# Graph attention and a mixture of experts on one core: weighted sums in pairs, and the shared steps in a new order

## The chip, the core and the metric
The kernel runs on one core of a Trainium2 chip. The metric is the device time of one execution in microseconds, lower is better. Engines: PE (TensorE: matmuls; its weight loads are listed apart as PEld), DVE (VectorE), ACT (ScalarE), POOL (GpSimd), SP (SyncE, here only a DMA queue and its waits). All five follow programs of their own and meet at semaphores.

## What is computed
Four graphs of 256 nodes go through two layers of an 8-head graph attention, which updates `x`; then every token goes to two of 16 experts and to a shared expert. Cut to what matters:

```python
def gat_layer(x, adj, W, a_self, a_neigh, b):
    feat = jnp.einsum('nf,hfo->hno', x, W)
    e = (feat*a_self).sum(-1)[:, :, None] + (feat*a_neigh).sum(-1)[:, None, :]
    e = leaky_relu(e, 0.2) + MASK_VAL * (1.0 - adj)
    return elu(softmax(e) @ feat + b)                 # heads side by side
x = x + tanh(g_xattn) * gat_layer(gat_layer(ctx, layernorm(x), ...), ...)
flat = layernorm(x);  logits = flat @ router_w.T     # top 2 of 16, with weights
for e in range(16): out += combine[:, e] * (silu(flat@Wu[e]) * (flat@Wg[e])) @ Wd[e]
out += (silu(flat @ Su) * (flat @ Sg)) @ Sd            # the shared expert
x = x + tanh(g_ffn) * out
```

## The kernel before
**Attention.** The work is cut into eight units, (graph, layer): four graphs of layer 0, then four of layer 1. A unit has four pairs of heads. For pair `j` of unit `k`, PE's `edges(k, j)` spreads the row terms into one of two PSUM banks, DVE's `edge` turns them into masked, unnormalised weights in `prob` (two operations a head, some 0.41 us each), and PE's `weighted(k, j)` multiplies them with the features into `ps_pv`. The two heads of a pair use the two halves of the array's columns, 64 apart, side by side. `prob` has four slots for a head each, so DVE's write for pair `j` waits for the sums of pair `j - 2`; an `edges` waits for DVE to have read the pair two before it.

Between these lies the rest of the neighbouring units: `own_maxima(k+1)` (one column, after DVE's row maxima), `turn_pv(k-1)` (eight transpositions of the sums of the unit before), `features(k+1)`, `spread_t(k+1)`, `rows(k+2)` (projections) and `turn_z(k-1)` (only where the unit before is of layer 0). ACT's order in unit `k` is fixed: `evict_h1` (the turned output of two units ago, behind `turn_z`), `evict_pv(k-1, 1)` (the upper half of the sums, out of PSUM), `row_exps(k+1)` (seven small operations in a chain), ELU, three evictions, `evict_pv(k, 0)`. POOL then makes `rows_r`, for which the next unit's first `edges` waits. `turn_pv` waits for both halves of `evict_pv`:

```python
def turn_pv(k):
    for half in range(2):
        pe.wait_ge(pv_out[half], k + 1)
```
The loop runs over units 0 to 5; units 6 and 7 are written out, interleaved with normalisation and router of the first graphs.

**Router.** For each graph, `route`, DVE's top two, `ranks` (PE counts who came before) and `positions` give each token a row in a DRAM table; POOL scatters the tokens there. After graph 3 DVE makes the table of tiles (`tables`), PE turns it (`turn_table`), `whole_tables` writes it as integers, SP reads it and loads the first tiles, once the scatters have landed. `warm(n)` are `n` idle matmuls.

**Shared expert.** Eight steps `s`, two for a graph: `up(s)` on PE, `gate_tanh(s)` on ACT, `shared_step(s)` on DVE (two operations), `down(s)` on PE into `ps_acc`. Steps 0 to 3 run among the router's work, 4 to 7 behind the expert tiles. `base(g)` adds the result of graph `g` to `x_res`.

**Tiles and tail.** 24 tiles of two experts' 64 rows each; then each token's two results are read back (`y_got`), `bring(g, k)` adds them on DVE, and SP stores.

Of the kernel before, what the change touches and what calls it, by code (L numbers as in the profile page):

```python
# [13 lines left out]
P = 128  # L14
HEADS, F_OUT = 8, 32
# [21 lines left out]
def flamingo_block(nc, x, ctx_t, gates, w0, w1, a_self, a_neigh, b0, b1, router_t, router_bias,  # L37
# [13 lines left out]
    EARLY = SHARED_STEPS // 2  # L51
# [12 lines left out]
    with ExitStack() as ctx:  # L64
        def sb(name, shape, dt=F32):
            return ctx.enter_context(nc.sbuf_tensor(name, shape, dt))
# [4 lines left out]
        def sem(name):  # L71
# [66 lines left out]
        prob = sb("prob", [P, 4, C, N])  # L138
# [60 lines left out]
        y_got = [t[:].rearrange("p a c n -> p (a c n)").rearrange("p (g k f) -> p g k f", g=2, k=TOP)[:, i]  # L199
                 for t in (prob, mask_t) for i in range(2)]  # L200
# [320 lines left out]
        def _(act):  # L521
# [216 lines left out]
            gate_tanh(2)  # L738
            gate_tanh(3)
# [10 lines left out]
            for s in range(EARLY, SHARED_STEPS - 2):  # L750
                gate_tanh(s)
# [4 lines left out]
            for s in range(SHARED_STEPS - 2, SHARED_STEPS):  # L756
                gate_tanh(s)

        @block.vector
        def _(dve):  # L760
# [96 lines left out]
            def edge(k, h):  # L857
                a, i = UNITS[k]
                n = HEADS * k + h
                dve.wait_ge(edge_ready, n // 2 + 1)  # L860
                if h == 0:
                    dve.wait_ge(t_nat_ready, k + 1)
                    dve.wait_ge(mask_t_ready, a + 1)
                if n >= 4:
                    dve.wait_ge(pv_done, n // 2 - 1)
                for c in range(C):
                    last = dve.scalar_tensor_tensor(prob[:, n % 4, c, :], ps_edge[n // 2 % 2][:, h % 2, :],  # L867
                                                    t_nat[:, k % 2, c, 0, h:h + 1], mask_t[:, a, c, :],
                                                    ALU.max, ALU.mult)
                last.then_inc(p_done, 1)  # L870
# [274 lines left out]
            for j in range(W_AHEAD):  # L1145
                pick_weights(j, of_tile[j])
            base(1)
# [8 lines left out]
            for s in range(EARLY, SHARED_STEPS - 1):  # L1156
                shared_step(s)
# [3 lines left out]
            shared_step(SHARED_STEPS - 1)  # L1161
# [3 lines left out]
            base(B - 1, range(T - 1))  # L1165
# [5 lines left out]
        def _(pe):  # L1171
# [80 lines left out]
            def weighted(k, j):  # L1252
                n = PAIRS * k + j
                pe.wait_ge(p_done, 2 * (n + 1))
                if j == 0:
                    pe.wait_ge(feat_ready, k + 1)
                    if k == 0:
                        pe.wait_ge(pv_zeroed, 1)
                if j % 2 == 0 and k:
                    pe.wait_ge(pv_out[j // 2], k)  # L1260
                for c in range(C):
                    for h in range(2 * j, 2 * j + 2):
                        at = 64 * (h % 2)
                        last = pe.matmul(ps_pv[at:at + HO, j, :], feat[:, k % 2, c, h, :],  # L1264
                                         prob[:, (HEADS * k + h) % 4, c, :], start=(c == 0), stop=(c == C - 1))
                last.then_inc(pv_done, 1)
# [57 lines left out]
            def task(k, j):  # L1324

                before, after, later = k - 1, k + 1, k + 2
                if j == 0 and 0 <= before < NU:
                    turn_pv(before)
                if j == 1 and after < NU:
                    features(after)  # L1330
                    spread_t(after)
                if j == 1 and k in MASK_SLOT:
                    turn_mask(MASK_SLOT[k])
                if j == 2 and later < NU:
                    rows(later)
                if j == 3 and graph_after(before, 0) is not None:
                    turn_z(before, graph_after(before, 0))

            def up(s, ks=range(2)):
                g, e = s // SHARED, EXPERTS + s % SHARED  # L1340
                if EARLY <= s < EARLY + 2:
                    pe.wait_ge(h_done, TILES)
# [38 lines left out]
            def tile_up(j):  # L1381
                pe.wait_ge(picked, j + 1)
                pe.wait_ge(xt_out, j + 1)
                if j >= 2:
                    pe.wait_ge(h_done, j - 1)
                for c in range(C):
# [110 lines left out]
            down(2)  # L1497
            warm(8)
            turn_tile(0)
            down(3)  # L1500
            for j in range(TILES + 2):
# [8 lines left out]
                if 0 <= j - 2 < TILES:  # L1510
                    tile_down(j - 2)
            for s in range(EARLY, SHARED_STEPS):
                up(s)
                if s > EARLY:
                    down(s - 1)
            down(SHARED_STEPS - 1)
# [51 lines left out]
```

## Time and profile before
| what | value |
|---|---|
| median of 3 runs | 206.76 us (202.15 to 207.87) |
| the profiled execution | 201.63 us, of which the span of instructions is 199.5 us |
| PE | 172.8 us busy, 87% of the span |
| DVE | 153.5 us, 77% |
| ACT | 96.1 us, 48% |
| POOL | 79.8 us, 40% |
| mean granted TensorE clock | 0.978 |
| chain that ended last | PE 70%, DVE 17%, issue 5% |

The share of busy time is a mean over stages with different limits: attention (to 104 us, with the router of the first graphs inside its last units), router and shared steps (to 134 us), tiles (to 182 us) and tail. The start and the length of single operations come from the timeline; an x8 behind a row joins eight instructions of one line, and its length is that from the first one's start to the last one's end. A matmul of 32-bit floats shows as two passes, so `weighted` shows as x8, `up` as x8 and `down` as x4. The time in square brackets is how long the engine stood idle before, and what released it.

### The profile page before, as it was taken

The page shows a single profiled execution, that of the slowest core. Times are in us where ns is not written, and L with a number is a line of the kernel's source. Part 1 is how long each engine was busy: PE and PEld are TensorE (multiplying, and loading weights), DVE is VectorE, ACT ScalarE, POOL GpSimd, SP SyncE. Part 2 cuts the span into 40 slices and gives each one's busy share as a digit, 9 for nine tenths or more (in the row PEclk, how much of TensorE's full clock was granted, in tenths as well). Part 3 has the DMA queues.
Part 4 walks back from the last instruction along what each step waited for, and adds up shares of the span by engine and source line. Part 5 has one row for each costly group of instructions (what it writes and reads, how often), then busy time and mean ns, then how long its engine had stood idle before and what let it go on. Part 6 is the DMA issues. An engine that isn't in the chain of part 4 may idle for free.

```text
span 199.5 us, 4043 instructions
## 1 busy us (share of the span) xinstructions
PE 172.8 (87%) x1137; PEld 115.1 (58%) x1137; DVE 153.5 (77%) x491; ACT 96.1 (48%) x252; POOL 79.8 (40%) x116
## 2 busy tenths in 40 slices
PE   0286999999999999998997985499999999998962
PEld 0065456566767675665765774395555555545841
DVE  6986999989989899989997875728676676740494
ACT  2063647594888383866118320005566565653100
POOL 8067563512141414342275574300545455455000
PEclk9999999999999999999999999679999999999997
DMA  3799999999999940000031021223444444411684
GB/s 128 216 395 430 424 420 424 416 414 424 288 357 350 412 194 0 3 0 2 0 109 55 14 102 71 83 80 81 132 150 129 147 126 146 127 61 79 184 316 158
DMA packets 18358, 38.13 MB, mean 191 GB/s; under 512 B 2785, under 2 KB 13602, under 8 KB 16162
## 3 DMA queue, kind: packets, MB, share of 16 engines
q1 hardware_dynamic: 15488, 31.25, 43.7%
q0 software_dynamic: 1920, 5.26, 7.0%
q10 hardware_dynamic: 930, 1.38, 1.9%
q8 instruction: 9, 0.15, 0.3%
q14 instruction: 11, 0.09, 0.1%
HBM read 14.53 MB, written 23.35 MB: 190 GB/s over the span
## 4 chain that ended last, share of the span: by engine, by line
PE 70%; DVE 17%; issue 5%; ACT 3%; POOL 2%; another core or an unknown queue 1%; POOLq 0%; DVEq 0%; ACTq 0%
PE ps_pv L1264 15%; PE ps_edge L1389 12%; PE ps_edge L1248 6%; PE ps_pv L1410 5%; PE ps_nat L1378 4%; PE ps_edge L1347 4%; PE ps_feat L1228 4%; PE ps_nat L1275 4%; DVE prob L867 3%; PE ps_rows L1211 2%; PE ps_nat L1190 2%; PE ps_nat L1185 2%; PE ps_pv L1358 2%; DVE x_res L1050 2%; PE ps_nat L1237 1%
## 5 line engine op out<-in xcount | busy, mean ns | idle before, releaser
L867 DVE SCALAR_TENSOR_TENSOR prob<-ps_edge,t_nat,mask_t 128x256 f32<-128x256 f32 x128 | 54.0, 477 | 3.3 <-PE ps_edge L1248 2.3
L487 POOL DMA_INDIRECT y_tok<-pv_t,y_row x24 | 23.1, 963 | 33.8 <-DVE y_row L1018 21.5
L1264 PE MATMUL ps_pv<-prob,feat 128*33 128x256 f32 x256 | 35.2, 397 | 0.6 <-issue 0.5
L1389 PE MATMUL ps_edge<-up_w,xt 128*64 x96 | 25.9, 392 | 0.0
L1389 PE MATMUL ps_edge<-up_now,xt 128*64 128x256 f32 x96 | 25.9, 392 | 0.0
L1264 PEld LDWEIGHTS ps_pv<-prob,feat 128*33 128x33 f32 x256 | 12.5, 113 | 12.3 <-issue 4.1
L1248 PE MATMUL ps_edge<-rows_r,sel_row 128*128 128x256 f32 x64 | 16.7, 348 | 1.8 <-DVE prob L867 1.5
L416 POOL TENSOR_TENSOR rows_r<-rows_q,rows_h 128x256 fp32r<-128x256 f32 x8 | 5.9, 731 | 30.9 <-ACT rows_h L549 30.9
L479 POOL DMA_INDIRECT x_rows<-x_hat,pos x12 | 12.2, 1019 | 10.2 <-DVE pos L955 7.1
L1248 PEld LDWEIGHTS ps_edge<-rows_r,sel_row 128*128 128x128 f32 x64 | 10.3, 205 | 9.8 <-issue 5.3
L1347 PE MATMUL ps_edge<-x_t,up_w 128*128 128x256 f32 x64 | 15.5, 385 | 0.0
L1389 PEld LDWEIGHTS ps_edge<-up_w,xt 128*64 128x64 f32 x96 | 11.2, 136 | 7.4 <-issue 3.8
L1410 PE MATMUL ps_pv<-down_w,x_less 128*64 x48 | 14.4, 381 | 1.1 <-issue 0.6
L670 ACT ACTIVATE xt<-ps_nat 128x256 f32<-128x256 f32 x24 | 9.1, 379 | 12.4 <-PE ps_nat L1378 12.2
L1034 DVE SCALAR_TENSOR_TENSOR mask<-mask,ps_edge 128x128 f32<-128x128 f32 x24 | 6.9, 287 | 10.0 <-ACT mask L676 9.3
L1410 PE MATMUL ps_pv<-down_now,x_less 128*64 128x256 f32 x48 | 14.4, 381 | 0.0
L688 ACT ACTIVATE pv_t<-ps_pv,mask_t 128x256 f32<-128x256 f32 x24 | 11.4, 475 | 5.1 <-PE ps_pv L1410 3.4
L676 ACT ACTIVATE mask<-ps_edge 128x128 f32<-128x128 f32 x24 | 6.7, 278 | 14.0 <-PE ps_edge L1389 8.2
L1347 PEld LDWEIGHTS ps_edge<-x_t,up_w 128*128 128x128 f32 x64 | 11.8, 190 | 2.6 <-issue 1.2
L569 ACT ACTIVATE pv_t<-ps_pv 128x512 f32<-128x512 f32 x16 | 9.5, 597 | 6.8 <-PE ps_pv L1264 6.8
L1025 DVE COPY up_now<-up_w 128x512 f32 x24 | 10.1, 421 | 1.8 <-issue 1.8
L1358 PE MATMUL ps_pv<-down_w,a_all 128*128 128x256 f32 x32 | 9.6, 425 | 2.2 <-issue 1.3
(188 smaller groups left out, 381.6 us busy)
## 6 DMA issues: line engine op xcount, KB each, us to landing
x_rows<-x_t SPq DMA_DIRECT2D x16, 1024.0 KB, 16.4
mask_t<-x_rows SPq DMA_DIRECT2D x48, 64.5 KB
up_w<-in_wu SPq DMA_DIRECT2D x1, 2048.0 KB, 30.3
up_w<-in_wg SPq DMA_DIRECT2D x1, 2048.0 KB, 11.2
down_w<-in_wd SPq DMA_DIRECT2D x1, 2048.0 KB, 10.1
x_res<-in_x SPq DMA_DIRECT2D x3, 256.0 KB, 3.7
out<-x_res SPq DMA_DIRECT2D x3, 256.0 KB, 2.1
prob<-y_tok SPq DMA_DIRECT2D x2, 256.0 KB, 3.4
```

The costliest lines, as they stand in the source:

```text
L479: pool.indirect_dma_start(x_rows[:], bass.IndirectOffsetOnAxis(pos[:, a, k, t:t + 1], 0), rows_of[a][:, k, t, :], None).then_inc(scattered ...
L487: pool.indirect_dma_start(y_tok[:], bass.IndirectOffsetOnAxis(y_row[:, j % R_SLOTS:j % R_SLOTS + 1], 0), y_sb[:, j % Y_SLOTS, :], None).th ...
L569: act.activation(pv_t[:, 2 * half:2 * half + 2], ps_pv[:, 2 * half:2 * half + 2], ACT.Copy).then_inc(pv_out[half], 1)
L688: act.activation(y_sb[:, j % Y_SLOTS], ps_y[j % 2], ACT.Copy, scale=x_in[:, j % X_SLOTS, D + 1:D + 2]).then_inc(y_ready, 1)
L867: last = dve.scalar_tensor_tensor(prob[:, n % 4, c, :], ps_edge[n // 2 % 2][:, h % 2, :], t_nat[:, k % 2, c, 0, h:h + 1], mask_t[:, a, c, ...
L1025: mark(dve.tensor_copy(up_now[:, j % W_SLOTS].rearrange("p k f -> p (k f)"), up_w[:, bass.ds(e, 1), :, :].rearrange("p s k f -> p (s k f)")))
L1248: last = pe.matmul(ps_edge[n % 2][:, h % 2, :], sel_row[:, h, :], rows_r[:, k % 2, :], start=True, stop=True)
L1264: last = pe.matmul(ps_pv[at:at + HO, j, :], feat[:, k % 2, c, h, :], prob[:, (HEADS * k + h) % 4, c, :], start=(c == 0), stop=(c == C - 1))
L1347: last = pe.matmul(ps_edge[s % 2][:, k, :], up_w[:, e, k, c * P:(c + 1) * P], x_t[:, g, c, :], start=(c == 0), stop=(c == C - 1))
L1358: last = pe.matmul(ps_acc[g % 2][:, t, :], hid_out[:, s % 2, t * P:(t + 1) * P], down_w[:, e, :], start=(s % SHARED == 0 and t == 0), stop ...
L1389: last = pe.matmul(ps_edge[j % 2][rows_at, 0, :].rearrange("p (k f) -> p k f", k=2), xt[:, j % 2, c, rows_at], up_w[:, bass.ds(experts[j], ...
L1410: last = pe.matmul(ps_y[j % 2][rows_at], ht_r[:, j % 2, rows_at], down_w[:, bass.ds(experts[j], 1), :] if i == 0 else down_now[:, j % W_SL ...
```

## The change
It does five things. (1) In units 0 to 5 the sums of pairs 0 and 1 come behind one another on PE, and so do those of pairs 2 and 3; the other pieces are placed around them anew. (2) `prob` gets eight slots, one for a head, and DVE waits for the sums of the same head one unit ago. (3) `up(3)` goes ahead of `ranks(3)`. (4) Steps 4 and 5 of the shared expert are begun (`up`, tanh, `shared_step`) before the tiles; their `down` stays behind the tiles. DVE's `shared_step(2)` goes ahead of `tables`, `shared_step(3)` ahead of `whole_tables`. (5) In the tail PE does `up(6)`, `up(7)` and then `down(4)` to `down(7)`; `base(3)` for the first half comes after `bring(0, ·)`.

```diff
-        prob = sb("prob", [P, 4, C, N])
+        prob = sb("prob", [P, HEADS, C, N])
...
-                if n >= 4:
-                    dve.wait_ge(pv_done, n // 2 - 1)
+                if k:
+                    dve.wait_ge(pv_done, n // 2 - PAIRS + 1)
...
             for k in range(NU - 2):
-                for j in range(PAIRS):
-                    if j + 2 < PAIRS:
-                        edges(k, j + 2)
-                    if j == 0:
-                        own_maxima(k + 1)
-                    weighted(k, j)
-                    if j + 2 >= PAIRS:
-                        edges(k + 1, j + 2 - PAIRS)
-                    task(k, j)
+                edges(k, 2)
+                own_maxima(k + 1)
+                if k:
+                    turn_pv(k - 1)
+                edges(k, 3)
+                weighted(k, 0)
+                weighted(k, 1)
+                edges(k + 1, 0)
+                spread_t(k + 1)
+                features(k + 1)
+                if k in MASK_SLOT:
+                    turn_mask(MASK_SLOT[k])
+                edges(k + 1, 1)
+                rows(k + 2)
+                weighted(k, 2)
+                weighted(k, 3)
+                if graph_after(k - 1, 0) is not None:
+                    turn_z(k - 1, graph_after(k - 1, 0))
...
             down(1)
-            warm(2)
+            up(3)
             ranks(3)
-            up(3)
-            warm(8)
+            warm(5)
+            down(2)
+            up(4)
             turn_table()
+            up(5)
+            down(3)
             pe.wait_ge(table_i_ready, 1)
...
-            down(2)
-            warm(8)
+            warm(6)
             turn_tile(0)
-            down(3)
...
+            for s in range(BEGUN, SHARED_STEPS):
+                up(s)
             for s in range(EARLY, SHARED_STEPS):
-                up(s)
-                if s > EARLY:
-                    down(s - 1)
-            down(SHARED_STEPS - 1)
+                down(s)
...
             positions(3)
+            shared_step(2)
             tables()
-            shared_step(2)
+            shared_step(3)
             whole_tables()
             base(0)
-            shared_step(3)
+            shared_step(4)
```
`BEGUN` is 6, `EARLY` 4. The old `task(k, j)` called `turn_pv(k-1)` behind `weighted(k, 0)`, `features` and `spread_t` behind `weighted(k, 1)`, `rows(k+2)` behind `edges(k+1, 0)` and `turn_z` at the end.

**PE in unit 4 before**, from its third `edges` to that of unit 5. L1248 is `edges`, L1217 `own_maxima`, L1264 `weighted`, L1275 `turn_pv`, L1228 `features`, L1237 `spread_t`, L1211 `rows`, L1190 `turn_z`:
```order
L1248 MATMUL ps_edge<-rows_r,sel_row 128x256 x2
L1217 MATMUL ps_rows<-row_max,shift 128x1
L1264 MATMUL ps_pv<-prob,feat 33x256 x4
L1275 MATMUL ps_nat<-ident,pv_t 128x128 x8
L1248 MATMUL ps_edge<-rows_r,sel_row 128x256 x2
L1264 MATMUL ps_pv<-prob,feat 33x256 x4
L1228 MATMUL ps_feat<-w_raw,h_t 128x256 x4
L1237 MATMUL ps_nat<-pick,rows_q 128x24 x2
L1264 MATMUL ps_pv<-prob,feat 33x256 x4
L1248 MATMUL ps_edge<-rows_r,sel_row 128x256 x2
L1211 MATMUL ps_rows<-h_t,w_rows 128x256 x2
L1264 MATMUL ps_pv<-prob,feat 33x256 x4
```
**PE in unit 4 after**, the same stretch:
```order
L1248 MATMUL ps_edge<-rows_r,sel_row 128x256 x2
L1217 MATMUL ps_rows<-row_max,shift 128x1
L1275 MATMUL ps_nat<-ident,pv_t 128x128 x8
L1248 MATMUL ps_edge<-rows_r,sel_row 128x256 x2
L1264 MATMUL ps_pv<-prob,feat 33x256 x8
L1248 MATMUL ps_edge<-rows_r,sel_row 128x256 x2
L1237 MATMUL ps_nat<-pick,rows_q 128x24 x2
L1228 MATMUL ps_feat<-w_raw,h_t 128x256 x4
L1248 MATMUL ps_edge<-rows_r,sel_row 128x256 x2
L1211 MATMUL ps_rows<-h_t,w_rows 128x256 x2
L1264 MATMUL ps_pv<-prob,feat 33x256 x8
L1190 MATMUL ps_nat<-ident,att 128x128 x4
```
`turn_pv` has lost the sums that stood between it and `own_maxima`, and the next unit's first `edges` (the third L1248) now stands ahead of `features` and `spread_t`.

**PE behind the ranks of graph 3** (L1313 is their last matmul), before. L1347 is `up`, L1358 `down`, L1185 `warm`, L1321 `turn_table`, L1491 PE's reading of the table:
```order
L1313 MATMUL ps_rows<-seen,ones 128x16
L1347 MATMUL ps_edge<-x_t,up_w 128x256 x4
L1185 MATMUL ps_nat<-ident 128x128 x8
L1321 MATMUL ps_feat<-ident,table 1x128 x2
L1491 TENSOR_LOAD table_i
L1358 MATMUL ps_pv<-down_w,a_all 128x256 x2
L1185 MATMUL ps_nat<-ident 128x128 x8
```
The same place after, where `up` is L1332, `down` L1343 and the reading L1490:
```order
L1313 MATMUL ps_rows<-seen,ones 128x16
L1185 MATMUL ps_nat<-ident 128x128 x5
L1343 MATMUL ps_pv<-down_w,a_all 128x256 x2
L1332 MATMUL ps_edge<-x_t,up_w 128x256 x4
L1321 MATMUL ps_feat<-ident,table 1x128 x2
L1332 MATMUL ps_edge<-x_t,up_w 128x256 x4
L1343 MATMUL ps_pv<-down_w,a_all 128x256 x2
L1490 TENSOR_LOAD table_i
L1185 MATMUL ps_nat<-ident 128x128 x6
```
`down(2)` and `up(4)` now stand between the ranks and `turn_table`, `up(5)` and `down(3)` between it and the reading.

## Rows read from the trace of the kernel before

**Rows 1.** Ten-microsecond stretches: busy time of PE, PEld, DVE, ACT, POOL, then granted clock.
```profile
20.00:30.00 10.00, 9.77 (x58) 5.32 (x58) 9.86 (x28) 5.74 (x15) 5.71 (x10) 1.00 1.01 424
...
60.00:70.00 10.00, 10.00 (x74) 6.80 (x72) 8.74 (x23) 5.86 (x15) 3.09 (x3) 1.00 1.10 385
```

**Rows 2.** Timeline, PE alone, unit 4: start us, duration us, operation.
```profile
58.95 0.48 PE L1248 MATMUL ps_edge<-rows_r,sel_row 128*128 128x256 f32 x2
...
59.48 1.06 PE L1264 MATMUL ps_pv<-prob,feat 128*33 128x256 f32 x8
...
60.47 1.09 PE L1275 MATMUL ps_nat<-ident,pv_t 128*128 128x128 f32 x8
...
61.73 1.06 PE L1264 MATMUL ps_pv<-prob,feat 128*33 128x256 f32 x8
...
62.72 2.00 PE L1228 MATMUL ps_feat<-w_raw,h_t 128*128 128x256 f32 x8
...
68.97 0.48 PE L1248 MATMUL ps_edge<-rows_r,sel_row 128*128 128x256 f32 x2
```

**Rows 3.** Timeline, PE in the expert tiles: staying in and leaving half-width matmuls.
```profile
176.75 0.38 PE L1410 MATMUL ps_pv<-down_now,x_less 128*64 128x256 f32 x1
...
176.96 0.38 PE L1410 MATMUL ps_pv<-down_now,x_less 128*64 128x256 f32 x1
...
177.27 0.33 PE L1400 MATMUL ps_feat<-ident,x_less 128*128 128x128 f32 x1
```

**Rows 4.** Timeline, ScalarE and GpSimd in the same unit 4.
```profile
59.23 0.60 ACT L587 ACTIVATE h_t<-ps_nat 128x512 f32<-128x512 f32 x1 [0.53 <-PE ps_nat L1190]
...
59.73 0.59 ACT L569 ACTIVATE pv_t<-ps_pv 128x512 f32<-128x512 f32 x1
...
60.20 0.27 ACT L531 ACTIVATE t_over<-ps_rows,row_max 128x1 f32<-128x1 f32 x1
...
62.98 0.73 POOL L416 TENSOR_TENSOR rows_r<-rows_q,rows_h 128x256 fp32r<-128x256 f32 x1 [4.69 <-ACT rows_h L549]
```

**Rows 5.** Timeline, end of unit 5 and of the loop.
```profile
74.87 0.75 DVE L889 SCALAR_TENSOR_TENSOR x_res<-att,gate,x_res 128x512 f32<-128x512 f32 x1
...
77.32 1.06 PE L1264 MATMUL ps_pv<-prob,feat 128*33 128x256 f32 x8
...
79.12 1.06 PE L1275 MATMUL ps_nat<-ident,pv_t 128*128 128x128 f32 x8 [0.31 <-issue]
```

**Rows 6.** Timeline, from unit 1 to unit 2.
```profile
36.43 1.65 DVE L867 SCALAR_TENSOR_TENSOR prob<-ps_edge,t_nat,mask_t 128x256 f32<-128x256 f32 x4
...
39.25 0.51 PE L1248 MATMUL ps_edge<-rows_r,sel_row 128*128 128x256 f32 x2
```

**Rows 7.** Timeline, between router and expert tiles.
```profile
121.52 0.22 DVE L951 TENSOR_TENSOR placed<-onehot,ps_rows 128x64 f32<-128x64 f32 x1 [2.05 <-remote]
...
122.55 0.96 POOL L479 DMA_INDIRECT x_rows<-prob,pos  x1 [2.23 <-DVE pos L955]
...
125.93 1.01 PE L1321 MATMUL ps_feat<-ident,table 128*1 128x128 f32 x4 [3.43 <-DVE table L975]
...
129.23 6.73 SPq L344 DMA_DIRECT2D mask_t<-x_rows  x9
...
134.47 0.43 PE L1389 MATMUL ps_edge<-up_w,xt 128*64 x1
```

**Rows 8.** One microsecond there, columns as in the first group.
```profile
126.00:127.00 1.00, 0.94 (x4) 0.27 (x4) 0.70 (x3) 0.00 (x0) 0.69 (x2) 0.50 0.36 132
```

**Rows 9.** Timeline, the tail behind the last expert tile.
```profile
181.94 3.72 PE L1347 MATMUL ps_edge<-x_t,up_w 128*128 128x256 f32 x16
...
189.61 0.68 DVE L1012 TENSOR_TENSOR x_res<-ps_pv,x_res 128x512 f32<-128x512 f32 x1
...
191.60 0.42 DVE L1001 SCALAR_TENSOR_TENSOR w_prod<-a_all,ps_edge 128x256 f32<-128x256 f32 x1
...
192.06 0.48 DVE L1005 SCALAR_TENSOR_TENSOR a_all<-w_prod,half_gate,ps_edge 128x256 f32<-128x256 f32 x1
```

More of the change, by code:

```diff
@@ L198, in flamingo_block @@
         y_sb = pv_t
-        y_got = [t[:].rearrange("p a c n -> p (a c n)").rearrange("p (g k f) -> p g k f", g=2, k=TOP)[:, i]
-                 for t in (prob, mask_t) for i in range(2)]
+        y_got = [t.rearrange("p a c n -> p (a c n)").rearrange("p (g k f) -> p g k f", g=2, k=TOP)[:, i]
+                 for t in (prob[:, 0:4], mask_t[:]) for i in range(2)]
         ps_edge = [psum(f"ps_edge{i}", [P, 2, N]) for i in range(2)]
@@ L737, in _ @@
             route_exp(3)
-            gate_tanh(2)
-            gate_tanh(3)
+            for s in range(2, BEGUN):
+                gate_tanh(s)
             tile_xt(0)
@@ L749, in _ @@
                     tile_y(j - 2)
-            for s in range(EARLY, SHARED_STEPS - 2):
+            for s in range(BEGUN, SHARED_STEPS):
                 gate_tanh(s)
@@ L755, in _ @@
                 act.dma_start(y_got[g][:, 1], y_view[g][:, T * D:2 * T * D]).then_inc(y_landed[g][1], 16)
-            for s in range(SHARED_STEPS - 2, SHARED_STEPS):
-                gate_tanh(s)
         @block.vector
@@ L863, in edge @@
                     dve.wait_ge(mask_t_ready, a + 1)
-                if n >= 4:
-                    dve.wait_ge(pv_done, n // 2 - 1)
+                if k:
+                    dve.wait_ge(pv_done, n // 2 - PAIRS + 1)
                 for c in range(C):
-                    last = dve.scalar_tensor_tensor(prob[:, n % 4, c, :], ps_edge[n // 2 % 2][:, h % 2, :],
+                    last = dve.scalar_tensor_tensor(prob[:, h, c, :], ps_edge[n // 2 % 2][:, h % 2, :],
                                                     t_nat[:, k % 2, c, 0, h:h + 1], mask_t[:, a, c, :],
@@ L1146, in _ @@
                 pick_weights(j, of_tile[j])
+            shared_step(5)
             base(1)
@@ L1155, in _ @@
             settle()
-            for s in range(EARLY, SHARED_STEPS - 1):
+            for s in range(BEGUN, SHARED_STEPS):
                 shared_step(s)
@@ L1160, in _ @@
                 bring(0, k)
-            shared_step(SHARED_STEPS - 1)
+            base(B - 1, range(T - 1))
             for g in (1, 2):
@@ L1164, in _ @@
                     bring(g, k)
-            base(B - 1, range(T - 1))
             for k in range(TOP):
@@ L1264, in weighted @@
                         last = pe.matmul(ps_pv[at:at + HO, j, :], feat[:, k % 2, c, h, :],
-                                         prob[:, (HEADS * k + h) % 4, c, :], start=(c == 0), stop=(c == C - 1))
+                                         prob[:, h, c, :], start=(c == 0), stop=(c == C - 1))
                 last.then_inc(pv_done, 1)
@@ L1322, in turn_table @@
                 last.then_inc(table_turned, 1)
[L1324 to L1337, printed above, removed]
             def up(s, ks=range(2)):
                 g, e = s // SHARED, EXPERTS + s % SHARED
-                if EARLY <= s < EARLY + 2:
+                if BEGUN <= s < BEGUN + 2:
                     pe.wait_ge(h_done, TILES)
@@ L1385, in tile_up @@
                     pe.wait_ge(h_done, j - 1)
+                else:
+                    pe.wait_ge(ug_read, BEGUN - 1 + j)
                 for c in range(C):
@@ L1511, in _ @@
                     tile_down(j - 2)
+            for s in range(BEGUN, SHARED_STEPS):
+                up(s)
             for s in range(EARLY, SHARED_STEPS):
-                up(s)
-                if s > EARLY:
-                    down(s - 1)
-            down(SHARED_STEPS - 1)
+                down(s)
             add_results()
```

2 lines of the change are left out of this document (1 added, 1 removed).

## Prediction
> **What bounds the kernel now.** I read the ten-microsecond stretches first. In units 3 and 4 PE is busy all the time, 10.00 of 10 us, and DVE 8.74; in units 0 and 1 it is the other way round, DVE 9.86 and PE 9.77 [rows 1]. Then the timeline of unit 4. It lasts from PE's third `edges` at 58.95 to the next one at 68.97, 10.02 us, with no hole on PE [rows 2]. Beside it ACT and POOL work in a chain that PE does not feel yet: `evict_h1` at 59.23, `evict_pv` at 59.73 (ready at 60.32), the seven `row_exps` from 60.20, and `rows_r` ready at 62.98 + 0.73 = 63.71 [rows 4]. Last the stretch before the tiles, where scatters and the table set the time [rows 7], and the tail, where DVE's additions do [rows 9].
>
> **Weighted sums in pairs: what they save.** A `weighted` takes 61.73 to 62.72, 0.99 us, for four passes of two heads side by side [rows 2]. In the tiles a half-width pass follows the one before after 0.21 us, but a full-width matmul follows it after 0.31 us [rows 3]. Four passes of 0.21 us are 0.85 us, so 0.10 to 0.15 us of the 0.99 are spent on getting into and out of half-width work. Two of four such visits go in each unit. With the entry behind `spread_t`, which goes as well, I take 0.3 us a unit, 0.2 to 0.5.
>
> The row shows a price of leaving. The Trainium skill (TensorEngine Tiling (Array Packing), Key Properties) has the rule for it: a change of the tiling mode, not of the tile alone, drains TensorE. By that rule alone the change must make each PE-bound unit faster, and that is the second rival below.
>
> **What they cost: a new wait for ACT.** Before, `weighted(k, 0)` stood between `own_maxima` and `turn_pv`. ACT's `evict_pv` was ready at 60.32 and `turn_pv` began at 60.47, the moment the sums were through (59.48 + 0.99) [rows 2, 4]. These sums hid the eviction almost exactly. Now only `edges(k, 2)` and `own_maxima` are ahead of it, 59.48 - 58.95 = 0.53 us. Counted from the third `edges` as zero:
> - `evict_h1` begins at 0.28, since `turn_z` still ends just before zero; `evict_pv` is ready at 1.37 [rows 4]. ACT's order is the old one. `turn_pv` begins at 1.42 instead of 0.53: PE waits 0.89 us.
> - `turn_pv` and `edges(k, 3)` take 61.73 - 60.47 = 1.26 us, to 2.68. The four half-pairs of sums take 0.99 + 0.99 - 0.13 = 1.85 us, to 4.53.
> - Next comes the new unit's first `edges`, which was some 7 us in and is now at 4.5. It needs `rows_r`, ready at 63.71 - 58.95 = 4.76. It begins at 4.81: another 0.28 us.
> - The rest has the same pieces as the 68.97 - 62.72 = 6.25 us before, less 0.2 for the visit saved: 6.05. The unit ends at 10.86.
>
> So 10.86 for 10.02, 0.84 us more. Both waits come out of the same chain, which starts with `turn_z`; PE being late moves it along, so nothing is caught up. `turn_pv` waits behind nothing but PE itself, and behind it are `edges(k, 3)`, all sums and the next `edges`, hence DVE. DVE has room: its 8.74 of 10 us fit into 10.86. The eight slots take away DVE's wait for the sums two pairs ago, but DVE isn't the bound here, so this is worth nothing.
>
> Units 2, 3 and 4 have a `turn_z` ahead of them and pay 0.84 each, **+2.5**. Unit 5 pays it too. Besides, DVE's extra addition of 0.75 us there [rows 5] makes the last edge ready at some 7.65 where PE is at 7.35, +0.3. Behind the loop `turn_pv(5)` follows its sums directly. Before, it began at 79.12, 0.8 us behind the end of the sums (77.32 + 0.99), 0.35 of it `edges` [rows 5]; now it waits some 0.75 us for ACT, +0.3. Unit 5: **+1.4**.
>
> Units 0 and 1 follow DVE. Before, DVE was through with unit 1 at 36.43 + 0.83 = 37.26, and unit 2 began on PE 2.0 us later, at 39.25 [rows 6]. Now the last `edges` comes first and has to wait for DVE, then `rows`, two pairs of sums and `turn_z`: 0.35 + 0.6 + 1.85 + 0.35 = 3.15 us. (`edges`, `rows` and `turn_z` are estimates from 0.23 us for a pass of 256 columns, 3.66 us by 16 [rows 9].) With 0.2 because DVE's row maxima wait for the later `rows`: **+1.4**, between 0.3 and 2. Units 6 and 7 are as before; DVE gets to them further ahead, **-0.3**. Attention in all: **+5.0** (3 to 6.5).
>
> **Between router and tiles.** `up(4)`, `up(5)` fill time in which PE waits 3.43 us for the table [rows 7]. Ahead of `turn_table` DVE now does `shared_step(2)`, 0.42 + 0.48 us [rows 9], so the table is turned at 126.85 for 125.93, and DVE writes its integers behind `shared_step(3)`, at about 128.0. SP would have the numbers at 129.3; before, its first load went out at 129.23, held by the scatters [rows 7]. So the load is not later by more than 0.1. The tiles began at 134.47, 5.24 us behind the load [rows 7], after idle matmuls and `down(3)` at or near half clock; the clock had fallen to 0.50, 1.2 GHz, behind the wait [rows 8]. `down(3)` is out of the way now (0.9 us at full clock, four passes of 0.23), two idle matmuls fewer, but DVE has a step more to do (0.9) before `base(1)`. I take **-0.5**, from -1.3 to +1.2.
>
> In the same rows stands something that I can't explain: DVE waited 2.05 us for the ranks of graph 3, to 121.52, released by nothing that the profile names. POOL's last scatters began at 122.55 for it, after 2.23 us of idling [rows 7]. If it goes, all of this is up to 2 us earlier.
>
> **Tail.** Before, PE did four `up` (1.83 us each) and four `down`; two `up` are now gone, 3.66 us of PE. But DVE sets the end. Its `base(2)` began at 189.61 and it worked on from there to the end, with a shared step of 0.9 us within [rows 9]. Now: `up(6)`, `up(7)` to 181.94 + 3.7 = 185.65, `down(4)`, `down(5)` 0.92 each to 187.5, the last half of `shared_step(7)` 0.48 behind it, since it overwrites what `down(5)` reads: `base(2)` at 188.1, 1.5 earlier. The step within is gone, 0.9 more. The read-back of the tokens' results doesn't start earlier and could take 0.5 of it back. **-1.9**, from -2.4 to -0.8.
>
> **Sum.** +5.0 - 0.5 - 1.9 = +2.6 us. The profiled execution took 201.63 us, so 204.2 in its place. The median is 206.76 and the fastest of the three 202.15; the profiled one is like the fastest. I add to the median: **209.4 us**.
>
> **Rivals.**
> 1. *The unnamed wait of 2.05 us goes*, because `ranks(3)` stands elsewhere. For it: DVE and PE were both past their work, and the ranks' own matmuls are tiny. Against it: nothing shows that the order made it. The sum is then +0.6, 207.4.
> 2. *PE does not wait for ACT*, and only the switches count: I would have misread which operation holds `turn_pv`. Then 5 PE-bound units save 0.2 to 0.3, -1.2, and the whole is -1.2 - 0.5 - 1.9 = -3.6: 203.2. The rule of the Trainium skill on draining gives this. With rival 1 on top it is 201.1. Against it: the 0.15 us between ACT's end and `turn_pv`'s start.
> 3. *Slower by more than 2%: the clock falls under `up(4)`.* PE stands still from the ranks to `down(2)`, some 3 us, not much less than the 3.43 us behind which the clock stood at 0.50 [rows 7, 8]. At half clock `down(2)` and `up(4)` take 5.5 instead of 2.75 us and `turn_table` comes 1.8 us or more after the table. The load goes out some 2 us late, of which the missing `down(3)` gives back 0.9. With +1.2 for -0.5 the sum is +4.3: 211.1. It decides where `up(4)` ends behind the table, at about 126.8. The Trainium skill (TensorE: Matmul & The Clock Gate, Why this matters for your kernels) warns of idle gaps between bursts of matmuls for the same reason.
> 4. *The change doesn't reach PE's bound at all*, since DVE holds all units: 206.76 - 2.4 = 204.4. The 8.74 us speak against it.
>
> **How the numbers follow.** Forecast 0.42 (its own range 207 to 211), rival 1 0.2, rival 2 0.14, rival 3 0.14, rival 4 0.1. A measurement of this kernel tells about 2% from no change, that is 202.6 and 210.9. Faster by more than that: half of rival 2, the low end of 1 and 4, 0.14. Slower: rival 3 and the high end of the forecast, 0.22. Within: 0.64. The range is 202.3 to 212.0.
>
> **What would show it.** In the changed profile: PE's `turn_pv` idle by 0.7 to 0.9 us before it in units 2 to 5, released by ACT's `pv_t`; the first `edges` of a unit idle by 0.3, released by POOL's `rows_r` or ACT; a unit of 10.8 us instead of 10.0; sums of x16 in 1.85 us; DVE's share in the units lower than before; `base(2)` 1.5 us nearer to the last tile. I would be wrong if ACT's eviction had been ready earlier than its row says, if leaving half-width work cost much more than 0.15 us, or if the clock behaved differently before the tiles.

## The result, and the profile after
The changed kernel took 206.16 us (median of 4 runs, 205.79 to 209.96) beside 204.87 us for the kernel before; the ratio is 1.016, 95% interval 1.012 to 1.021. Run again later beside the kernel before it was 206.34 us for 200.97, ratio 1.031 (1.024 to 1.039). It is slower both times, by 1.6 and by 3.1 percent; the two intervals don't meet, so the size of the loss also hangs on something other than the order of the code. Some executions of either kernel took about 4 us more, and the ratios leave them out, while the medians hold them. The profiled execution took 206.18 us with a span of 204.4 us, for 201.63 and 199.5: the change costs 4.9 us of span. That is one execution of each, and the one of the kernel before was faster than any of the four in its median.

Followed through the two traces, the loss is made in attention and a fifth of it comes back behind:

| place | before | after | later by |
|---|---|---|---|
| third `edges` of unit 2 | 39.25 | 40.99 | 1.74 |
| of unit 3 | 48.92 | 52.13 | 3.21 |
| of unit 4 | 58.95 | 62.92 | 3.97 |
| of unit 5 | 68.97 | 73.71 | 4.74 |
| `turn_pv(5)` | 79.12 | 85.25 | 6.13 |
| DVE behind the ranks of graph 3 | 121.52 | 127.64 | 6.12 |
| first load of a tile | 129.23 | 135.79 | 6.56 |
| first `tile_up` | 134.47 | 140.38 | 5.91 |
| `up` behind the tiles | 181.94 | 187.84 | 5.90 |
| end of the last addition | 197.37 | 202.28 | 4.91 |

The stretches that answer to [rows 1], in the kernel after. In 60 to 70 us PE was busy for 10.00 us and DVE for 8.74; now it is 8.94 and 7.90:
```profile
20.00:30.00 10.00, 9.15 (x52) 5.07 (x52) 9.36 (x26) 5.09 (x13) 5.72 (x10) 1.00 1.01 424
60.00:70.00 10.00, 8.94 (x67) 6.16 (x66) 7.90 (x20) 8.09 (x18) 3.09 (x3) 1.00 1.11 380
```
The timeline of PE in unit 4 after, for [rows 2] (L1248 `edges`, L1275 `turn_pv`, L1264 the sums). Both waits stand in the brackets:
```profile
62.92 0.48 PE L1248 MATMUL ps_edge<-rows_r,sel_row 128*128 128x256 f32 x2
...
64.38 1.06 PE L1275 MATMUL ps_nat<-ident,pv_t 128*128 128x128 f32 x8 [0.87 <-ACT pv_t L570]
65.20 0.48 PE L1248 MATMUL ps_edge<-rows_r,sel_row 128*128 128x256 f32 x2
65.62 1.92 PE L1264 MATMUL ps_pv<-prob,feat 128*33 128x256 f32 x16
67.73 0.51 PE L1248 MATMUL ps_edge<-rows_r,sel_row 128*128 128x256 f32 x2 [0.19 <-POOL rows_r L417]
...
73.71 0.48 PE L1248 MATMUL ps_edge<-rows_r,sel_row 128*128 128x256 f32 x2
```
The unit takes 73.71 - 62.92 = 10.79 us. Its two waits are 1.06 us, and 10.79 - 1.06 = 9.73 against 10.02 before, so PE's work in the new order is 0.29 shorter. Not all of that is the joining: the second joined set takes 1.85 us (71.45 to 73.30) for 2 x 0.99, and `features`, which no longer follows half-width sums, takes 1.62 (68.44 to 70.06) for 1.83 (62.72 to 64.55). ACT and POOL in the same unit, for [rows 4]:
```profile
63.20 0.60 ACT L588 ACTIVATE h_t<-ps_nat 128x512 f32<-128x512 f32 x1
63.69 0.59 ACT L570 ACTIVATE pv_t<-ps_pv 128x512 f32<-128x512 f32 x1
...
66.94 0.73 POOL L417 TENSOR_TENSOR rows_r<-rows_q,rows_h 128x256 fp32r<-128x256 f32 x1 [4.17 <-ACT rows_h L550]
```
The eviction is ready at 64.28 and `turn_pv` begins at 64.38; `rows_r` is ready at 67.67 and the edges begin at 67.73. Counted from the third `edges` both stand where they stood before (1.36 for 1.37 us, 4.75 for 4.76).

Between router and tiles, for [rows 7], timeline (L950 the first operation behind the ranks, L480 the first scatter of graph 3, L1343 `down(2)`, L1332 `up(4)`, L1321 `turn_table`), and the clock under `up(4)`, third number from the end, for [rows 8]:
```profile
127.64 0.22 DVE L950 TENSOR_TENSOR placed<-onehot,ps_rows 128x64 f32<-128x64 f32 x1 [2.08 <-remote]
128.66 0.96 POOL L480 DMA_INDIRECT x_rows<-prob,pos  x1 [2.35 <-DVE pos L954]
129.28 1.13 PE L1343 MATMUL ps_pv<-down_w,a_all 128*128 128x256 f32 x4 [2.58 <-DVE a_all L1004]
...
130.24 3.47 PE L1332 MATMUL ps_edge<-x_t,up_w 128*128 128x256 f32 x8
...
133.64 0.66 PE L1321 MATMUL ps_feat<-ident,table 128*1 128x128 f32 x4
```
```profile
131.00:132.00 1.00, 1.00 (x4) 0.81 (x3) 0.86 (x6) 0.00 (x0) 0.81 (x1) 0.50 0.42 144
```
The unnamed wait is there again. PE stands still for 2.58 us; `down(2)` then still runs at the full clock, and `up(4)` runs at 0.50 of it, 1.2 GHz, for most of its 3.47 us.

The tail, for [rows 9], timeline:
```profile
187.84 3.72 PE L1332 MATMUL ps_edge<-x_t,up_w 128*128 128x256 f32 x16
...
191.40 3.67 PE L1343 MATMUL ps_pv<-down_w,a_all 128*128 128x256 f32 x16
...
193.80 0.68 DVE L1011 TENSOR_TENSOR x_res<-ps_pv,x_res 128x512 f32<-128x512 f32 x1
...
199.08 1.61 DVE L1049 TENSOR_TENSOR x_res<-mask_t,x_res 128x512 f32<-128x512 f32 x3 [0.68 <-DMA mask_t<-y_tok]
199.75 2.07 PE L1354 MATMUL ps_pv<-mask_t,ident 128*128 128x256 f32 x4 [4.68 <-DMA mask_t<-y_tok]
...
201.86 0.42 DVE L1058 TENSOR_TENSOR x_res<-ps_pv,x_res 128x256 f32<-128x256 f32 x1 [1.18 <-PE ps_pv L1354]
```
`base(2)` (193.80) is 5.96 us behind the first `up`, for 7.67 before. But now DVE and PE both wait for the read-back of the tokens' results. L1354 is `add_results`; the granted clock under it is 0.50. In the kernel before it ran at 1.00, behind DVE and not behind the read-back:
```profile
195.81 1.10 PE L1369 MATMUL ps_pv<-mask_t,ident 128*128 128x256 f32 x4 [2.09 <-DVE x_res L1012]
```

### The profile page after: what moved, and what is told of

It is laid out like the page before. It is cut to its first block, busy times and chain, and to the rows that moved or that the text cites. A ratio compares the mean times of both kernels' runs of the same rounds, so it can differ in the third digit from the quotient of the medians.

```text
span 204.4 us, 4011 instructions
## 1 busy us (share of the span) xinstructions
PE 169.8 (83%) x1123; PEld 113.5 (56%) x1123; DVE 152.2 (74%) x491; ACT 96.4 (47%) x252; POOL 79.6 (39%) x116
## 4 chain that ended last, share of the span: by engine, by line
PE 48%; DVE 15%; issue 14%; ACT 7%; DMA 5%; POOL 5%; SPq 2%; another core or an unknown queue 1%; POOLq 0%; DVEq 0%; ACTq 0%
PE ps_edge L1376 12%; PE ps_pv L1264 8%; DVE prob L866 5%; PE ps_pv L1397 4%; PE ps_nat L1363 4%; DMA mask_t<-y_tok 3%; PE ps_edge L1332 3%; PE ps_edge L1248 3%; PE ps_feat L1228 2%; PE ps_nat L1190 2%; PE ps_nat L1275 1%; PE ps_rows L1211 1%; DMA y_tok<-pv_t,y_row 1%; POOL rows_r L417 1%; POOL feat L432 1%
## 5 line engine op out<-in xcount | busy, mean ns | idle before, releaser
L866 DVE SCALAR_TENSOR_TENSOR prob<-ps_edge,t_nat,mask_t 128x256 f32<-128x256 f32 x128 | 53.1, 475 | 3.1 <-ACT mask_t L607 1.8
L1264 PE MATMUL ps_pv<-prob,feat 128*33 128x256 f32 x256 | 33.2, 398 | 0.6 <-issue 0.5
L1264 PEld LDWEIGHTS ps_pv<-prob,feat 128*33 128x33 f32 x256 | 13.7, 114 | 14.1 <-issue 4.4
L1248 PE MATMUL ps_edge<-rows_r,sel_row 128*128 128x256 f32 x64 | 16.8, 350 | 5.6 <-DVE prob L866 4.4
L1248 PEld LDWEIGHTS ps_edge<-rows_r,sel_row 128*128 128x128 f32 x64 | 10.5, 205 | 12.0 <-DVE prob L866 5.5
L1332 PE MATMUL ps_edge<-x_t,up_w 128*128 128x256 f32 x64 | 17.1, 415 | 0.0
L480 POOL DMA_INDIRECT x_rows<-x_hat,pos x12 | 12.2, 1016 | 10.1 <-DVE pos L954 7.1
L1332 PEld LDWEIGHTS ps_edge<-x_t,up_w 128*128 128x128 f32 x64 | 12.6, 203 | 3.2 <-issue 1.4
L1275 PE MATMUL ps_nat<-ident,pv_t 128*128 128x128 f32 x64 | 8.5, 276 | 4.4 <-ACT pv_t L570 3.5
L432 POOL TENSOR_TENSOR feat<-feat_raw,feat 128x512 f32<-128x512 f32 x8 | 8.6, 1077 | 7.8 <-ACT feat_raw L556 7.5
```

The lines of the kernel that those rows point to most:

```text
L432: pool.tensor_tensor(feat[:, k % 2, :, :, 0:F_OUT], raw, weight.to_broadcast([P, C, HEADS, F_OUT]), ALU.mult).then_inc(feat_ready, 1)
L480: pool.indirect_dma_start(x_rows[:], bass.IndirectOffsetOnAxis(pos[:, a, k, t:t + 1], 0), rows_of[a][:, k, t, :], None).then_inc(scattered ...
L866: last = dve.scalar_tensor_tensor(prob[:, h, c, :], ps_edge[n // 2 % 2][:, h % 2, :], t_nat[:, k % 2, c, 0, h:h + 1], mask_t[:, a, c, :], ...
L1248: last = pe.matmul(ps_edge[n % 2][:, h % 2, :], sel_row[:, h, :], rows_r[:, k % 2, :], start=True, stop=True)
L1275: last = pe.transpose(ps_nat[:, t, j * P:(j + 1) * P], pv_t[:, j, t * P:(t + 1) * P], ident[:])
L1332: last = pe.matmul(ps_edge[s % 2][:, k, :], up_w[:, e, k, c * P:(c + 1) * P], x_t[:, g, c, :], start=(c == 0), stop=(c == C - 1))
```

## Experiments

### attn_only: the loop and the slots alone
```diff
 kernel before, and
-prob = sb("prob", [P, 4, C, N])
+prob = sb("prob", [P, HEADS, C, N])
 the loop over units 0 to 5 as after
```


> The kernel before with the attention loop and the eight slots of the change alone; ranks, shared steps and tail as before. Theory (waits for ACT and POOL in every unit, and units 0 and 1 turned round): the end of attention comes 6.1 us later, as in the changed kernel, and the whole is 5 to 6.5 us slower than before, 3 percent. Rival (the loop only saves switches of half-width work): 1 to 1.5 us faster. Rival (the loss in the changed kernel came from the new steps behind attention): within 1 us of before.

It was 207.6 us for 203.26, ratio 1.020 (1.015 to 1.026), some 4 us. The trace ends 6.8 us later than that of before. Third `edges` stood at 42.24, 53.38, 64.16, 74.95: units 3 and 4 take 10.78 and 10.79 us, as in the change. It reached unit 2 1.25 us later than the change did, because the clock fell once, from 37 to 41 us. One of these microseconds:
```profile
38.00:39.00 1.00, 1.00 (x4) 0.54 (x3) 0.36 (x1) 1.00 (x3) 0.00 (x0) 0.50 0.99 410
```
So the loop makes the whole loss, and the two rivals fall: it is not faster, and it is not within 1 us. The 4 us are less than the 5 to 6.5 expected, and `turn_pv(5)`, at 86.48, is 7.36 us later than before, for the 6.1 expected.

### slots_only: eight slots, nothing else
```diff
+prob = sb("prob", [P, HEADS, C, N])
+                if k:
+                    dve.wait_ge(pv_done, n // 2 - PAIRS + 1)
```


> The kernel before with eight slots for the edge terms and nothing else. Theory: DVE's write isn't held by the sums where PE is the bound, so within 0.3 us of before. Rival: DVE waited for a slot in units 0 and 1, which follow DVE; then up to 1 us faster. [...]

202.44 us for 203.26, ratio 0.996 (0.993 to 0.999). The third `edges` of units 3 and 4 stood at 49.33 and 59.36, 10.03 apart as before. By the interval the slots gain between 0.1 and 1.4 us, where I had expected less than 0.3. The rival, a wait for a slot in units 0 and 1, would fit the time, but in the trace unit 2 begins 0.4 us later than before, at 39.66 for 39.25, so it isn't shown. The loss isn't theirs.

### act_swap: ACT evicts the sums first
```diff
-                if h == 0 and graph_after(k - 2, 0) is not None:
+                if h == 1 and graph_after(k - 2, 0) is not None:
                     evict_h1(graph_after(k - 2, 0))
-                if h == 1 and 0 <= before < NU:
+                if h == 0 and 0 <= before < NU:
                     evict_pv(before, 1)
```


> The changed kernel, on ACT the upper half of evict_pv stands ahead of evict_h1. Theory (turn_pv waits 0.87 us because evict_pv stands behind evict_h1, 0.6 us, which itself waits for turn_z): the wait ahead of turn_pv falls to at most 0.3 us in units 2 to 5; evict_h1 is 0.1 to 0.3 us later and so is rows_r, so the wait of the first edges grows from 0.19 to 0.4 to 0.9 us. A unit then takes 10.3 to 10.5 for 10.79 us, the whole is 1.2 to 2 us faster than the changed kernel. Rival (rows_r sets the unit): the second wait takes all of it, unit stays 10.8, within 0.4 us.

205.13 us, ratio 1.010 (1.006 to 1.015) where the change had 1.016; its span is 2.0 us shorter than that of the change. These two ran on different chips and the intervals of their ratios overlap, so I go by the units: from unit 2 to 5 they took 10.67, 10.31, 10.65 and 11.07 us for 11.14, 10.79, 10.79 and 11.54, 1.56 us less in all. The wait ahead of `turn_pv` did not fall to 0.3, and its name changed. Timeline, ACT and PE, unit 3, then PE in unit 4:
```profile
52.32 0.60 ACT L588 ACTIVATE h_t<-ps_nat 128x512 f32<-128x512 f32 x1
...
53.17 1.06 PE L1275 MATMUL ps_nat<-ident,pv_t 128*128 128x128 f32 x8 [0.54 <-ACT h_t L588]
```
```profile
63.84 1.06 PE L1275 MATMUL ps_nat<-ident,pv_t 128*128 128x128 f32 x8 [0.89 <-ACT h_t L588]
```
`turn_pv` writes the same PSUM tensor `ps_nat` that `evict_h1` has yet to read, and the code makes it wait for that. Both evictions hold it, in either order. The swap only lets the first one run under `turn_z`, and in unit 4 ACT came late from four operations on `x_res` (2.55 us from 59.58), so that nothing was won at this place. The second wait, expected to grow, went: `rows_r` was ready 4.28 us into unit 3 and 4.63 into unit 4, for 4.75. The gain of 1.56 us lies in the 1.2 to 2 that I expected, but it comes by another way than I gave.

### turn_covered: pair 0's sums ahead of turn_pv again
```diff
                 own_maxima(k + 1)
+                weighted(k, 0)
                 if k:
                     turn_pv(k - 1)
                 edges(k, 3)
-                weighted(k, 0)
                 weighted(k, 1)
                 edges(k + 1, 0)
```


> The changed kernel with pair 0's sums ahead of turn_pv, as before; everything else stands as in the change, the next unit's first edges right behind the sums of pair 1. Theory (rows_r, 4.76 us into the unit, holds the first edges whatever stands ahead): the wait ahead of turn_pv goes, the one ahead of the first edges grows from 0.19 to 0.9 or 1.0 us, a unit stays at 10.7 to 10.9 us and the time within 0.5 us of the changed kernel. Rival (the wait ahead of turn_pv alone makes the loss): a unit of 10.0 us, 3 to 4 us faster than the changed kernel.

206.46 us, ratio 1.033 (1.028 to 1.039). Unit 3 took 10.79 us, unit 4 10.77. Timeline, PE, unit 4:
```profile
66.72 1.09 PE L1275 MATMUL ps_nat<-ident,pv_t 128*128 128x128 f32 x8
...
70.01 0.51 PE L1248 MATMUL ps_edge<-rows_r,sel_row 128*128 128x256 f32 x2 [0.97 <-POOL rows_r L417]
```
The first wait is gone and the second is as long as both were. This is the clearest run of the study: `rows_r`, 4.75 us into the unit, sets the unit as long as the next edges stand right behind the first two sums. Curing the larger of the two waits alone is worth nothing.

### edges_late: the next unit's first edges behind spread_t and features
```diff
                 weighted(k, 1)
-                edges(k + 1, 0)
                 spread_t(k + 1)
                 features(k + 1)
...
+                edges(k + 1, 0)
                 edges(k + 1, 1)
```


> The changed kernel with the next unit's first edges behind spread_t and features, directly ahead of its second. Theory (two waits out of one chain, the first ahead of turn_pv, the second for rows_r): the second, 0.19 us, goes, the first, 0.87 us, stays; a unit takes 10.5 to 10.65 us for 10.79, the whole is about 1 us faster than the changed kernel. Rival (DVE gets its next pair 2.5 us later and becomes the bound): a unit of 11 us or more, slower than the changed kernel.

205.5 us, ratio 1.031 (1.024 to 1.039) beside a before of 200.09. Units 3 and 4 took 10.51 and 10.53 us. Timeline, PE, unit 4:
```profile
64.32 1.07 PE L1275 MATMUL ps_nat<-ident,pv_t 128*128 128x128 f32 x8 [0.87 <-ACT pv_t L570]
...
69.49 0.83 PE L1248 MATMUL ps_edge<-rows_r,sel_row 128*128 128x256 f32 x4
```
The second wait goes, the first stays, and the unit is shorter by 0.27. By the units the gain is the one expected; against the change in microseconds it can't be told, since the two did not run on the same chip. The rival fell: the unit is not 11 us.

### half_pairs: join only the pairs whose neighbours don't wait
The new body of the loop; its conditions and `turn_mask` are left out here.
```diff
+                edges(k, 2)
+                own_maxima(k + 1)
+                weighted(k, 0)
+                turn_pv(k - 1)
+                edges(k, 3)
+                weighted(k, 1)
+                features(k + 1)
+                spread_t(k + 1)
+                edges(k + 1, 0)
+                rows(k + 2)
+                weighted(k, 2)
+                weighted(k, 3)
+                edges(k + 1, 1)
+                turn_z(k - 1)
```


> The changed kernel with another attention loop: pair 0's sums stand ahead of turn_pv again and pair 1's behind the fourth edges, as before, and only the sums of pairs 2 and 3 come behind one another, at the unit's end; the next unit's first edges come ahead of rows but behind features. Theory (a joined pair saves 0.13 us, the waits come only from turn_pv and the first edges being early): no wait of PE for ACT or POOL, a unit of 9.85 to 9.95 us, attention 0.3 to 1.0 us shorter than in the kernel before, the whole about 2.5 to 3 us faster than before. Rival (joining sums costs by itself, since DVE gets its edges later): unit 10.1 or more, slower than the kernel with the old loop and the new rest, 200.96 us.

198.48 us for 200.09, ratio 0.987 (0.982 to 0.992). Timeline, PE, unit 4:
```profile
58.30 0.48 PE L1248 MATMUL ps_edge<-rows_r,sel_row 128*128 128x256 f32 x2
...
59.81 1.09 PE L1275 MATMUL ps_nat<-ident,pv_t 128*128 128x128 f32 x8
...
65.53 1.92 PE L1264 MATMUL ps_pv<-prob,feat 128*33 128x256 f32 x16
67.39 0.51 PE L1248 MATMUL ps_edge<-rows_r,sel_row 128*128 128x256 f32 x2
...
68.09 0.48 PE L1248 MATMUL ps_edge<-rows_r,sel_row 128*128 128x256 f32 x2
```
No bracket, so no wait. The two joined sums take 67.39 - 65.53 = 1.86 us for 2 x 0.99 [rows 2], a saving of 0.12, and the unit is 9.79 for 10.02; another 0.09 comes from `spread_t`, which is followed by `edges` now and no longer by half-width sums (0.36 for 0.45). The ratio is worth 2.6 us, as expected. This version beats the kernel before and the changed one. But most of that is the new rest, which alone had 0.988 (`rest_only`, below): that the half-joined loop is better than the old one, only the traces show, where `turn_pv(5)` begins at 77.99 for 79.12 before and 79.03 in `rest_only`.

### rest_only: the change without its loop
```diff
 kernel after, with the loop and the four slots of before
```


> The changed kernel with the old attention loop and four slots: ranks, shared steps and tail in the new order alone. Theory (terms add up): middle -0.2 and tail -1.0 us, so 1.2 us faster than before, between 0.5 and 2.4. The unnamed wait of 2 us between the ranks' matmuls and DVE should be there again. Rival (the clock falls under up(4) as soon as the scatters are not late any more): 1 us or more slower than before.

200.96 us for 203.26, ratio 0.988 (0.980 to 0.997), and the trace ended 2.8 us earlier. At the places of the table above: load 0.28 earlier, first tile 0.93, `up` behind the tiles 0.83, end of the last addition 2.82, so the tail alone is 2.0 shorter. The unnamed wait was there (2.06 us), as expected, and the rival fell. The gain, 2.4 us by the ratio and 2.8 in the trace, is at or above the upper end of what I expected from the trace of the change, 1.2 (0.5 to 2.4): there `up(4)` and `add_results` ran at half the clock, 3.47 and 2.07 us, and here they took 1.89 and 1.33. So ranks, shared steps and tail are worth 1.2 to 2.8 us in the traces, and the loop spends more than that.

### scatter_split, after_again, before_again: the unnamed wait
```diff
 rest_only, and on POOL
-            scatter(2)
+            scatter(2, (0,))
             scatter(3)
+            scatter(2, (1,))
```


> The old attention loop with the new rest; POOL does only half of graph 2's scatters ahead of graph 3's and the other half behind them, so that its last scatter ahead of the unnamed wait ends 2.5 us earlier. Theory A (DVE's first instruction behind the ranks of graph 3 begins 1.2 us behind the end of POOL's scatters, as in six traces, or when the ranks are done): it begins within 0.4 us of the ranks' end instead of 2.06 us of idling, the last scatter ends 0.6 us later than in the kernel with the old loop. Theory B (it begins some 2 us behind the ranks whatever POOL does): idle 2.06 us again, last scatter and tiles 2.5 us later.

> The changed kernel once more, unaltered, to see it beside the others of this call. In the first traces DVE idled 2 us behind the ranks of graph 3 (the unnamed wait); in four traces taken on another chip it did not. Theory (the wait belongs to the chip or to the moment, not to the order of the code): it is here in this kernel and in the kernel before alike, or in neither; the attention part is as in the first trace, third edges at 40.99, 52.13, 62.92, 73.71 us within 0.1, and the ratio to before is 1.016 to 1.035. Rival (the order makes the wait): it is here again with 2.0 us, whatever the other kernels of this call show.

> The kernel before once more, unaltered. Theory (wait of the chip or the moment): DVE's first instruction behind the ranks of graph 3 idles 2 us exactly if it does so in the changed kernel of this call; if not, the tiles begin at about 132.5 us for 134.47. Rival (the order makes the wait): idle 2.05 us again, tiles at 134.4.

In `scatter_split` (203.1 us, one execution) DVE began 0.03 us behind the ranks (idle 0.20), which would fit theory A; but the three kernels run beside it on the same chip, with POOL's order unaltered, didn't have the wait either. So it tells nothing of POOL. What does is `after_again`: DVE began at 125.94, while POOL's last scatter of graph 2 ran from 125.79 to 126.75, so there at least DVE waits for no end of these scatters. The two unaltered kernels settle part of it. DVE's first instruction behind the ranks, in the kernel after and then in the kernel before, run on one chip:
```profile
125.94 0.22 DVE L950 TENSOR_TENSOR placed<-onehot,ps_rows 128x64 f32<-128x64 f32 x1 [0.17 <-PE ps_rows L1313]
```
```profile
120.08 0.22 DVE L951 TENSOR_TENSOR placed<-onehot,ps_rows 128x64 f32<-128x64 f32 x1 [0.45 <-PE ps_rows L1313]
```
Both kernels lose the wait together: the order of the code alone doesn't make it. `before_again` (201.07 us, one execution) began its tiles at 132.39, as expected for this case. In `after_again` the third `edges` stood at 41.60, 52.74, 63.52 and 74.30, 0.6 later than the first time and not within 0.1, the units being equal. Its load came 2.25 us earlier than the first time, but this was largely lost in the tiles:
```profile
138.00:148.00 10.00, 10.00 (x67) 5.04 (x66) 5.37 (x21) 4.61 (x16) 1.71 (x2) 0.83 0.32 87
```
There the clock stood at 0.83 over the first 10 us of the tiles and the tiles took 49.0 us for 47.5. That fits the higher ratio here, 1.031 for 1.016: the kernel before gained by the lost wait, the changed one gave it back, in this trace, in the tiles. One trace of each doesn't prove it.

### tail_warm and table_first: two repairs behind attention
```diff
 half_pairs, and behind the last down
+            warm(24)
             add_results()
```


> The kernel with pairs 2 and 3 joined and pairs 0 and 1 apart, and 24 idle matmuls between the last down and add_results. Theory (PE stands still 4.3 to 4.7 us ahead of add_results now that all downs come together, and its four matmuls then take 2.07 for 1.10 us at the lower clock, with the end of the kernel behind them): they take 1.1 us again, the end comes 0.7 to 1.0 us earlier, 1.5 to 2 percent faster than before in all. Rival (the end hangs on DVE's additions or on the last store): nothing moves, within 0.2 us of the kernel without them.

```diff
 tail_warm, and
-            up(4)
             turn_table()
+            up(4)
```


> As the one ahead of it, with turn_table ahead of up(4). Theory (the load of the first tiles hangs on the scatters, 1.85 us behind POOL's last, unless up(4) runs at the lower clock as it did in the changed kernel): within 0.3 us of the one ahead of it where DVE doesn't idle behind the ranks, and 0.3 to 0.5 us faster where it does. Rival (the table is the bound everywhere): 0.5 to 1 us faster in every case.

`tail_warm` gave 0.984 (0.977 to 0.991), `table_first` 0.990 (0.985 to 0.994), `half_pairs` 0.987: no difference that these runs can tell. They ran on another chip than `half_pairs`, so small gains would not show. Each idle matmul is two passes of 0.115 us, 5.52 us in all. Timeline of PE in `tail_warm`:
```profile
188.36 5.52 PE L1185 MATMUL ps_nat<-ident 128*128 128x128 f32 x48
...
194.14 1.13 PE L1354 MATMUL ps_pv<-mask_t,ident 128*128 128x256 f32 x4 [0.26 <-DMA mask_t<-y_tok]
```
The last matmuls take 1.13 us for 2.08 in `half_pairs`, so half of my theory holds. But `add_results` began 9.05 us behind the issue of the read-back (185.09), 9.27 in `table_first`, and 7.69 in `half_pairs`: the read-back landed that much later and took the gain. In the seven other traces with this tail and no idle matmuls it was 7.7 to 8.3 us. That fits a delay by the idle matmuls, but how they could make it isn't shown. `table_first` had no unnamed wait, and there nothing was to be gained, as the first theory had it; the case with the wait wasn't met.

## Why the prediction was right, and where it was off
The time forecast, 209.4 us, lies 3.2 above the 206.16 measured, and the sign is right. I had forecast +2.6 us, 1.3 percent, and given 0.64 to a change too small to tell; measured are 1.6 percent, which still lies within it, and 3.1 the second time, which doesn't. So the change costs more than I said, and that the time came out so near is in part luck: two errors stand against one another. The change costs 4.9 us in the spans, not +2.6; and the sum was added to a median of three runs, 206.76, which a fourth made 204.87, while the profiled execution stood at 201.63. By the profiled execution alone my sum would have said 204.2 for 206.18. The mechanism is not luck:

**The new wait for ACT** was predicted at 0.89 and is 0.87. The trace has it in every unit from 2 to 5, released as named. **The second wait**, for `rows_r`, 0.28, is 0.19. **The saving on half-width work**, 0.3 a unit, is 0.29, though a good part of it stands in `features` and not in the sums. **The unit**, 10.86, is 10.79. Units 3 and 4 cost 0.76 and 0.77 for 0.84, unit 5 1.39 for 1.4. `turn_covered` shows that the two waits come out of one chain, as I argued, and `edges_late` that the second goes when its edges stand later.

What of the waits I had not seen: `turn_pv` is held by `evict_h1` as well as by `evict_pv`, as `act_swap` shows. The forecast didn't suffer, since ACT does them in that order.

**Unit 2** is the term that was mis-sized: 1.47 for 0.84. The wait that the units behind it don't have is 0.51 us, of its last `edges` for DVE, which got there late from unit 1. **Units 0 and 1** gave 1.74 for 1.4, within the bounds. The reason given, the last `edges` waiting for DVE, shows as an idle of 1.67 us on PE at 35.68; beside it DVE waits 0.94 us at 38.74 for the turned mask, which I had not counted. **Units 6 and 7** gave nothing back for -0.3: `turn_pv(5)` is 6.13 and the operation behind the last ranks 6.12 us later. Attention is +6.1 for +5.0, inside its bounds of 3 to 6.5.

**Between router and tiles**: -0.2 for -0.5 in the first pair of traces, -0.7 in the second (turned sums 6.42 later, first tile 5.69). The load comes sooner ahead of the first tile, 4.59 us for 5.24; `before_again` had 4.59 without the change, so this part isn't the change's for certain. Rival 3, the clock falling under `up(4)`, did happen, but cost 0.3 to 0.6 us and not 1.8: the table, done at 132.31, was turned 1.3 us late, and the load began 2.38 us behind the end of POOL's last scatter, where the other traces have 1.7 to 2.1 (1.92 in [rows 7], from 126.35 + 0.96 to 129.23). In this trace the table is the bound: the load begins 1.21 us behind the integers, which are written at 134.58, and SP has no wait for the scatters, while in the kernel before it waits 0.6 us for them. The scatters would have held the load nearly as long, which hid the rest. Standing still isn't the whole cause of the fall: in `rest_only` PE stood still for 2.80 us at the same place, and `up(4)` took 1.89 us.

**Tail**: -1.0 for -1.9. The step was right up to `base(2)`, 1.71 us nearer for 1.5. What failed is the 0.5 that I allowed for the read-back: it costs 0.3 and 0.7 us of DVE's time, then the clock under `add_results`, whose four matmuls take 2.07 us behind 4.68 us of standing still, and took 1.10 in the kernel before. It is the read-back, and not DVE's additions, that the end hangs on now.

**Rivals.** 1 fell in this form: the wait stayed in the first traces, and where it goes it goes from both kernels. 2 fell: PE does wait for ACT. (Its saving of 1.2 us counts five PE-bound units; by [rows 1] and the units' lengths there are four, 2 to 5.) The rule of the Trainium skill on a drained array (TensorEngine Tiling (Array Packing), Key Properties) has the sign of the 0.29 us a unit, which it doesn't price; what it leaves out of the sum is who was hidden behind the sums. 4 fell: in 60 to 70 us DVE is less busy than before, 7.90 of 10 for 8.74.

## What to carry to other kernels
Work that seems only to separate two things may be hiding the latency of a third engine: before joining or moving it, write down, counted from one fixed point in the loop, when each waiting operation's input is ready, and keep every consumer behind that time. If two waits come out of one chain, curing the first alone only lengthens the second. Join what has nothing due next to it (here the last two pairs) and leave the rest; it is worth 0.23 us a unit in the trace here, too little for the timings to show.

## What the runs showed of the hardware
- In five traces (before, after, attn_only, rest_only, slots_only) DVE idled 2.02 to 2.08 us behind the ranks of graph 3 and began 1.6 to 2.6 us after their last matmul had ended; in four of them ACT, waiting for `up(3)`, went on within 0.1 us of DVE. In all five this was 1.15 to 1.33 us behind the end of POOL's scatters of graph 2 (in act_swap too, 1.20, but only 0.36 behind the ranks). In the eight traces from two other chips DVE began 0.03 to 0.04 us behind the ranks, in some of them before those scatters had ended. What makes the wait stays open.
- Two half-width sets of sums take 0.12 us less behind one another than with full-width work behind each (1.86 for 1.98 us).
- Standing still does not settle the clock by itself. The four matmul passes of `add_results` took 2.07 or 2.08 us behind 4.26 to 4.90 us of idle PE in seven traces, but 1.33, at a granted clock of 0.83, behind 4.41 in rest_only; behind 2.09 us of idling they took 1.10 in before and attn_only and 1.21 in before_again, but 2.05, at 0.50, in slots_only. Before the tiles `up(4)` took 3.47 us behind 2.58 of idling and one `down` in the changed kernel, but 1.89 behind 2.80 and one `down` in rest_only.
- The clock at the start of the tiles is not the same from run to run of one kernel: the first ten microseconds had 1.00 in one trace of the change and 0.83 in the other, worth 1.5 us.
